# TensorE sums both attention paths two beats behind their scores, in one place between the two score blocks

## The reference

```
q, k, v = split(x @ w_qkv.T);  k_y = x @ w_ky.T          # 16 heads of 16
agg = sum_k(exp(clip(q k_y / 4, -15, 15)) * causal) + EPS # "exponential path"
r   = log(|q k / 4| + EPS) - log(agg + EPS)
w   = softplus(r) * causal                                # = log(1 + (|L|+EPS)/(agg+EPS))
out = (w @ v) / (sum_k w + EPS);   x = layernorm(x + out @ w_proj.T)
```

## Time and profile before

| what | value |
|---|---|
| median of 3 runs | 1398.88 us (1397.62 to 1398.89) |
| the profiled execution | 1398.2 us; span from first to last instruction 1396.4 us |
| mean granted TensorE clock | 0.972 |
| TensorE busy | 1280.9 us, 92% |
| VectorE, ScalarE, GpSimd busy | 718.2, 614.8, 113.3 us |
| attention phase | to about 690 us |

### The profile page before, as it was taken

How to read it: one execution, slowest core, us unless ns; L and a number is a source line. 1 busy time by engine, 2 the same in 40 slices (tenths; PEclk the granted TensorE clock), 3 DMA queues, 4 the chain that set the end, 5 groups by cost and what they waited for, 6 DMA issues and landing times.

```text
span 1396.4 us, 22945 instructions
## 1 busy us (share of the span) xinstructions
PE 1280.9 (92%) x8310; PEld 817.6 (59%) x8310; DVE 718.2 (51%) x1223; ACT 614.8 (44%) x810; POOL 113.3 (8%) x140
## 2 busy tenths in 40 slices
PE   5888999999898989977399999999999999999996
PEld 1433444434343434433278778787787878878785
DVE  2456777677676776566243532535326353353523
ACT  3566666666666666655042322323223241232411
POOL 1111121111111121110000000000000000000000
PEclk8999999999999999998589999999999999999998
DMA  2002222132122221000290000000000000000000
GB/s 74 16 16 69 92 75 77 60 102 78 60 90 90 90 71 57 1 31 31 70 331 15 16 15 15 30 15 19 11 15 30 15 30 0 15 30 15 30 0 16
DMA packets 31943, 66.89 MB, mean 48 GB/s; under 512 B 2848, under 2 KB 8608, under 8 KB 31904
## 3 DMA queue, kind: packets, MB, share of 16 engines
q1 hardware_dynamic: 31904, 66.35, 14.3%
HBM read 46.42 MB, written 19.92 MB: 48 GB/s over the span
## 4 chain that ended last, share of the span: by engine, by line
issue 50%; POOL 0%; DVE 0%; POOLq 0%; DVEq 0%
POOL f_rstd L809 0%; DVE f_res L816 0%; POOLq L909 0%; DVEq L821 0%; POOL f_minus_half L907 0%; POOLq L83 0%
## 5 line engine op out<-in xcount | busy, mean ns | idle before, releaser
L935 ACT ACTIVATE f_h_full<-f_layer_bank,f_scales 128x512 f32<-128x512 f32 x128 | 88.0, 687 | 354.8 <-PE f_layer_bank L1049 354.7
L500 DVE TENSOR_TENSOR w_ring<-score_banks,keep 128x1024 int32<-128x1024 int32 (+1 forms) x192 | 191.6, 1040 | 46.9 <-PE score_banks L649 46.9
L353 ACT ACTIVATE e_ring<-score_banks 128x1024 f32<-128x1024 f32 (+1 forms) x192 | 158.8, 879 | 122.8 <-PE score_banks L649 122.0
L1049 PE MATMUL f_layer_bank<-f_ha_hi,f_w_all 128*128 128x512 f32 x512 | 204.7, 400 | 2.7 <-DVE f_h_full L977 2.3
L1049 PE MATMUL f_layer_bank<-f_hb_hi,f_w_all 128*128 128x512 f32 x512 | 202.8, 396 | 0.0
L1049 PE MATMUL f_layer_bank<-f_ha_lo,f_w_all 128*128 128x512 f32 x512 | 202.1, 395 | 0.0
L1049 PE MATMUL f_layer_bank<-f_hb_lo,f_w_all 128*128 128x512 f32 x512 | 202.0, 395 | 0.0
L491 DVE TENSOR_SCALAR e_ring<-e_ring 128x2048 f32<-128x2048 f32 (+1 forms) x96 | 100.5, 1046 | 122.3 <-ACT e_ring L353 122.3
L360 ACT ACTIVATE w_ring<-w_ring 128x2048 f32<-128x2048 f32 (+1 forms) x96 | 156.8, 1633 | 8.6 <-DVE w_ring L500 8.3
L287 POOL TENSOR_SCALAR_AFFINE_SELECT e_ring<-e_ring 128x512 f32<-128x512 f32 (+1 forms) x96 | 78.5, 818 | 516.5 <-DVE e_ring L491 516.5
L675 PE MATMUL acc_bank<-w_ring,v_aug 128*32 128x512 f32 (+3 forms) x1024 | 91.2, 452 | 27.8 <-ACT w_ring L360 27.8
(11 more groups left out here) (101 smaller groups left out, 1535.0 us busy)
## 6 DMA issues: line engine op xcount, KB each, us to landing
piece<-in_wf SPq DMA_DIRECT2D x44, 256.0 KB, 2.9
wf_copy<-piece SPq DMA_DIRECT2D x44, 256.0 KB, 3.0
f_w_all<-wf_copy SPq DMA_DIRECT2D x2, 4096.0 KB, 26.4
f_x_turn<-x SPq DMA_DIRECT2D x9, 512.0 KB, 3.2
xq<-in_xt SPq DMA_DIRECT2D x8, 512.0 KB, 3.3
xv<-in_xt SPq DMA_DIRECT2D x8, 512.0 KB, 3.3
res<-in_xn SPq DMA_DIRECT2D x8, 512.0 KB, 4.6
x<-res SPq DMA_DIRECT2D x8, 512.0 KB, 2.6
```

The source lines that it names most:

```text
L353: nc.scalar.activation(e_ring[:, t % RING, 2 * i:2 * i + 2, 0:cols], pair_banks(y_pair(t, i), cols), ACT.Exp).then_inc(exp_done, 1)
L500: nc.vector.tensor_tensor(w_ring[:, t % RING, 2 * i:2 * i + 2, 0:cols].bitcast(I32), pair_banks(w_pair(t, i), cols).bitcast(I32), keep[:, ...
L935: nc.scalar.activation(h_full[m % 2][:], f_bank[m % RING][:], ACT.Gelu, scale=scales[:, 1 + layer, m:m + 1]).then_inc(gelu_done, 1)
L1049: mm = nc.tensor.matmul(out, left.bitcast(dt), right.bitcast(dt), start=first and n == 0, stop=last and n == 1)
```

## The change

Four things are done. On TensorE the sums of both paths in beat t are those of beat t-2, and they stand together, after the first piece of misc work and before scores_w(t). The pieces of misc work are dealt out anew: flip_sums, spread_c and turn 0 come after scores_w, and turn 1, project_out and q_proj before the sums. ScalarE and VectorE get the matching order: the reads of the moved pieces stand after logs and after absolute. The copy of acc by ScalarE moves from the ends of beats 0 and 3 to beats 1 and 4.

```diff
-        def sums_of(t, y, w, before):
-            return before if t == 0 else (y, t - 1 in w)
-        def beat_before(k, t):
-            return (k, t - 1) if t else (k.shift(-1), BEATS - 1)
+        def beat_back(k, t, n):
+            return (k, t - n) if t >= n else (k.shift(-1), BEATS + t - n)
+        def in_beat_back(t, n, here, before):
+            return t - n in here if t >= n else before
...
 # ScalarE, in a beat, after exps(k, t) and v_sum_keep
+                    if t == 1 and out is not None:
+                        turn_keep(out, 1)
+                    if t == 1 and any(before):
+                        copy_sums(k.shift(-1), 1, before)
+                    if t == 3 and 3 in w:
+                        base_make(k.shift(-1))
+                    if t == 4 and project:
+                        q_keep(k.shift(1))
+                    if t == 4 and (y or 0 in w):
+                        copy_sums(k, 0, (y, 0 in w))
+                    if t == 5 and y:
+                        v_keep(k)
+                    if in_beat_back(t, 1, w, before[1]):
+                        logs(*beat_back(k, t, 1))
+                    if t == 0 and out is not None:
+                        turn_keep(out, 0)
                     if t == 1 and before[1]:
                         keep_att(k.shift(-1), 1, before[0])
+                    if t == 3 and project:
+                        ky_keep(k.shift(1))
                     if t == 4 and 0 in w:
                         keep_att(k, 0, y)
...
 # VectorE
-                    if t == 1 and before[0]:
-                        keep_agg(k.shift(-1), 1)
-                        factors(k.shift(-1))
-                    if t == 2 and 3 in w:
+                    if t == 3 and 3 in w:
                         qc_make(k.shift(-1))
-                    if t == 4 and y:
-                        keep_agg(k, 0)
                     if t == 1 and norm is not None:
                         norm_apply(nc, dve, norm, norm_tiles)
                     if y:
                         clip(k, t)
+                    if t == 2 and out is not None:
+                        residual(out, 0)
+                    if t == 3 and out is not None:
+                        residual(out, 1)
+                    if t == 4 and project:
+                        q_keep(k.shift(1))
                     if t in w:
                         absolute(k, t)
+                    if t == 1 and before[0]:
+                        keep_agg(k.shift(-1), 1)
+                        factors(k.shift(-1))
+                    if t == 4 and y:
+                        keep_agg(k, 0)
...
 # TensorE, after scores_y(k, t) and sum_values
+                    if t == 1 and out is not None:
+                        turn(out, 1)
+                    if t == 2 and out is not None:
+                        project_out(out, 0)
+                    if t == 3 and out is not None:
+                        project_out(out, 1)
+                    if t == 4 and project:
+                        q_proj(k.shift(1))
+                    if t == 5 and y:
+                        v_proj(k)
+                    if sums[0]:
+                        sum_exps(*beat_back(k, t, 2), not sums[1])
+                    if sums[1]:
+                        sum_weights(*beat_back(k, t, 2), not sums[0])
+                    if t in w:
+                        scores_w(k, t, y)
+                    if t == 0 and out is not None:
+                        turn(out, 0)
                     if t == 1 and any(before):
                         flip_sums(k.shift(-1), 1, before)
                     if t == 2 and 3 in w:
                         spread_c(k.shift(-1))
+                    if t == 3 and project:
+                        ky_proj(k.shift(1))
                     if t == 4 and (y or 0 in w):
                         flip_sums(k, 0, (y, 0 in w))
                     if t == 5 and y:
-                        v_proj(k)
...
+                        k_proj(k)
```

More of the change, by code:

```diff
@@ L411, in slot @@
                 for t in range(BEATS):
-                    sums = sums_of(t, y, w, before)
                     if y:
@@ L416, in slot @@
                         v_sum_keep(k.shift(-1))
+                    if t == 1 and out is not None:
[14 more added lines that the diff above has]
+                        turn_keep(out, 0)
                     if t == 1 and before[1]:
                         keep_att(k.shift(-1), 1, before[0])
-                    if t == 2 and 3 in w:
-                        base_make(k.shift(-1))
+                    if t == 3 and project:
+                        ky_keep(k.shift(1))
                     if t == 4 and 0 in w:
                         keep_att(k, 0, y)
[L423 to L432, removed]
                     if t == 5 and y:
@@ L436, in slot @@
                         piece_halve(k, t)
[L437 to L440, removed]
             natural_order(0)
@@ L571, in slot @@
                 for t in range(BEATS):
-                    if t == 1 and before[0]:
-                        keep_agg(k.shift(-1), 1)
-                        factors(k.shift(-1))
-                    if t == 2 and 3 in w:
+                    if t == 3 and 3 in w:
                         qc_make(k.shift(-1))
-                    if t == 3 and out is not None:
-                        residual(out, 1)
-                    if t == 4 and y:
-                        keep_agg(k, 0)
                     if t == 1 and norm is not None:
@@ L751, in slot @@
                 for t in range(BEATS):
-                    sums = sums_of(t, y, w, before)
-                    last = beat_before(k, t)
+                    sums = in_beat_back(t, 2, ALL if y else NONE, before[0]), in_beat_back(t, 2, w, before[1])
                     if y:
@@ L761, in slot @@
                         spread_c(k.shift(-1))
-                    if t == 3 and out is not None:
-                        project_out(out, 1)
+                    if t == 3 and project:
+                        ky_proj(k.shift(1))
                     if t == 4 and (y or 0 in w):
@@ L766, in slot @@
                     if t == 5 and y:
-                        v_proj(k)
[L768 to L780, removed]
                         k_proj(k)
-                    if sums[1]:
-                        sum_weights(*last, not sums[0])
             pe.wait_ge(kind_made, 3 * 2 * DT)
```

## The result

| | before | after |
|---|---|---|
| median | 1398.25 us (4 runs, 1394.01 to 1398.89) | 1444.78 us (4 runs, 1438.59 to 1448.15) |
| profiled execution, span | 1398.2, 1396.4 us | 1447.33, 1445.5 us |
| mean granted clock | 0.972 | 0.965 |

The ratio is 1.0334 (95% interval 1.029 to 1.0379): the change makes the kernel 46.5 us slower. The feed-forward phase is the same: from the first matmul of its layers to its last store it takes 694.0 us before and 693.4 after. That matmul starts at 699.1 and 748.8 us, 49.6 us later, so the whole loss of the profiled run (49.1 us) lies ahead of it, in attention.

A forecast was written before the change was run, and what follows sets the result against it. TensorE, 92% busy, bounds the kernel; attention slots with the output projection have almost nothing to win. Waits of +36.8 us and +1 for the clock, on 1398.2, give 1436 us; own range 1426 to 1446, 8 in 10 1402 to 1452.

The forecast's parts named there:

- rival (a): Granted clock falls once in each of 13 slots with both paths, up to 1.7 us each: +17, 1453 us; chance 0.12.
- six out slots: Slots carrying the output projection, with both paths: 44.97 us against 39.68 each, the last with fewer piece comparisons; +30.8 us.
- five slots of half 1: Loop slots without the output projection: 38.97 us against 38.53, the logarithm's saved wait spent on similar waits; +2.2 us.
- (1,0), (1,1): Slots of batch 1, both halves, with fewer pieces to cover waits: +0.7 us each.
- (7,1) and drain: Last slot with both paths, +0.7 us, and first slot without exponential-path scores, project_out waiting behind keep_att, +3.2 us.
- start and slot (0,1): Start of attention: two sums stop waiting for the masks, 1.5 of 2.3 us taken as gain.
- waits, together: All of the attention phase's slot, start and drain terms added: +36.8 us, matmul count and cost unchanged.
- clock: Granted clock may fall more often with more idle places over 1 us, partly landing in waits: only +1 us.
- First cost: Uncovered distance from scores_w to the next beat's scores: waits 0.82 us behind a transpose set, 1.41 in half 1's beat 0.
- Second cost: VectorE's chain of clip and absolute value sets short beats: beat 1 takes 5.61 us, waits 1.13 or 1.73 us.
- Third cost: Side-work bank read late: project_out waits 1.04 us for keep_att and 1.44 for qc_make, v_proj waits 1.04.
- The walk: Beat-by-beat reckoning of TensorE's work and waits in attention slots: 44.97 us with the output projection, 38.97 in half 1.

The follow-up runs named there:

- e3: The changed kernel with score blocks Y(2) of slots with the output projection and Y(5) of all slots computed twice into the same bank; 1431.24 us, ratio 1.0272.
- e2: The changed kernel with the weight sum, still two beats late, put back behind the beat's second score block; 1425.25 us, ratio 1.0228.
- e1: The changed kernel with VectorE's keep_agg ahead of absolute in beats 1 and 4; 1425.14 us, ratio 1.022; repeated, 1430.6 us.
- e5: e1 with VectorE's piece comparison of beat 2 moved behind qc_make; 1439.84 us, ratio 1.0279; repeated, 1435.21 us.

## Why the prediction was right, and where its size was off

It gave 1436 us and slower with 0.87; the time is 1444.78, inside 1402 to 1452 and near the upper end of its own narrower range, 1426 to 1446. It is no nearer to the forecast than to rival (a), 1453. By its terms, read in the profiled run (a slot's part without falls, taken from after's undisturbed slots and, for the last out slot, (1,1), (7,1) and the drain, from e3):

| term | forecast | measured |
|---|---|---|
| six out slots | +30.8 | +26.2 |
| five slots of half 1 | +2.2 | -0.4 |
| (1,0), (1,1) | +1.4 | +1.6 |
| (7,1) and drain | +3.9 | +2.4 |
| start and slot (0,1) | -1.5 | +2.3 |
| **waits, together** | +36.8 | +32.1 |
| **clock** | +1 | +17.5 |

The two sums missed in opposite directions, the waits by 4.7 us too much and the clock by 16.5 too little, so part of the closeness of the total is luck. What the fall in (0,1) cost is not known and stays in its row; before and e3 have falls in the drain too, and these stay in the row of the drain.

**First cost: right.** 0.82 forecast behind a transpose set, 0.76 measured; 1.41 in half 1, 1.35 measured; nothing behind a projection, none there. Only the 0.81 of beat 4 was too high, 0.53 measured. The wait for the absolute value is 53.3 against "some 45". e2 shows it is the distance from W to Y.

**Second cost: right.** Beat 1 was to be 5.61 and is 5.60.

**Third cost: right.** The three new rows on the side-work bank are those named: 1.01 for 1.04, 1.27 for 1.44, 0.92 for 1.04. e1 removes both waits for att_raw, e5 half of the one for qc (9.0 to 5.9 us over the run). e1 also shows what the prediction did not price: curing such a wait moves most of it to the score block, since VectorE's chain sets that beat. What the prediction says of the sums, that they never wait, is nearly so: 2.5 us in three places.

**The walk's small excess.** Two sums that follow each other were taken at 1.00 each. The rows at 427.87, 428.75 and 429.72 show 0.88 and 0.97: 1.85 for two. Four beats hang on such a pair, which makes 0.6 us per slot, and with the shorter wait of beat 4 the slot came out at 44.15 instead of 44.97. For the same reasons half 1 was not +0.4 but -0.1. Two slips in the text of the prediction did not touch its time: it speaks of 13 slots with both paths where its own sum has 14, and the 4.56 us per out slot in its bounds is not what the waits that it lists add up to.

**The start: wrong sign.** The sums' wait for the masks did go, but slot (0,1) is 1.9 us longer. Of these 1.0 are in beat 1, where a flip waits for the copy of acc, a wait that the prediction had not walked through; 0.4 are in beat 0, which has a long sum more, and the fall at 54.9 us lies in the slot too (TensorE's waits, 46 to 79 us):

```profile
PE misc_bank L707 <- ACT acc_copy L389: 2.1, 1, 2.1
```

**The clock: the term that was mis-sized.** The prediction had a fall in each of 13 slots as rival (a), 0.12, up to 1.7 us a fall, and put +1 in its sum, on the ground that some of it lands in waits. No run shows the +1, which was the author's estimate; the runs showed +17.5 in its place. The 1.7 is an estimate, half the length of a fall, of which the clock gave 0.51 (before, 204.6 to 208.0 us); 1.65 us were measured, so the price was right. The ground was wrong: in before a fall in a half-1 slot cost only 0.6 us (39.1 against 38.5), but after has its falls on projections and sums, behind which TensorE found too little wait to absorb them. Seven falls in out slots cost 11.2 us, those in (1,0) and (1,1) 3.0, less the 1.7 that before's three cost, and 5.0 more in the drain: 17.5. e3, which adds work and takes 13.5 us away, shows it. Rival (a), with +17 on top, had this part right. From before to after the falls grew from three to ten and the waits for the absolute value from 16.1 to 53.3 us, with no idle place over 1.35 us in the two slots of the loop shown above; but e1 has more wait at the scores (70.9 against 53.3) and no fall in the loop, and in after itself two out slots with the same waits have none, so idle time alone decides neither between kernels nor between slots.

**What stays open.** Behind which arrangement of short waits the clock falls. e1 and e5 differ by 0.6 us in one wait, and one has no fall in the loop, the other six or seven, in two profiles each. No run here tells why, and the number varies from run to run (after's four times spread over 9.6 us).

## What to carry to other kernels

Before moving a reader's work behind another engine's long instruction, walk the one shared buffer that it reads: its next writer can be late by up to that instruction, and three such waits (3.2 us in an out slot) are more than the 0.90 us wait for the logarithm that the change removed there. A wait removed at one end of a chain that another engine sets comes back at the next link; look for what stands needlessly ahead on the engine that sets it (norm_apply, 3.5 us in five slots) rather than for a later use. And price the clock apart from the waits: compare slots with and without a fall, in all parts of the run, and test with filler matmuls inside waits.

## What the runs showed of the hardware that was not expected

- More work, less time: filler score blocks inside existing waits took 13.5 us off (1444.78 to 1431.24), by holding the granted clock at 1.00 from 150 to 610 us instead of 0.97.
- A fall of 3.4 us to a granted clock of 0.50 to 0.51 cost 1.65 us on a projection in an out slot, 1.5 to 1.6 in a slot of half 1 of e5, and 0.5 to 0.6 in a slot of half 1 of before, which has waits behind it. In these it was what stood behind the fall that made the difference, not the kind of slot.
- A shorter wait can come with more time: with the comparison moved behind qc_make the kernel was 4.6 us slower than e1 on the same chip and 14.7 across chips, and 4.8 faster than e3 across chips. Out slots were 0.6 us shorter in both; the falls made the difference in the traces.
- Two 32-column sums that follow each other on different inputs start 0.88 us apart (427.87, 428.75), and the score block behind them starts 0.97 after the second, where the prediction had taken 1.00 for each from the rows of before.
